# One audio-tower layer on one core: the shared expert fed from stored transposed halves, early output rows, and a new order of the first stage

## What is computed

```
h = gelu(x[:, 1:] @ W1 + x[:, :1] @ W2 + b)               # W = tok_W, 512 x 256
z = layernorm(h);   q, k, v = z Wq^T, z Wk^T, z Wv^T       # 16 heads of 64
h = h + softmax(q k^T / 8) v Wo^T + bo                     # 255 keys
z = layernorm(h);   probs = softmax(z @ router)            # 8 experts, best two, not rescaled
routed = sum over the two of prob_e * (silu(z @ w1[e]) @ w2[e])
shared = sigmoid(z @ gate_w) * ((silu(z @ gate) * (z @ up)) @ down)
out = h + routed + shared                                  # 16 x 255 x 256
```

## Time and profile before

| | |
|---|---|
| three runs | 1058.63, 1057.09, 1057.47 us; median 1057.47 |
| the profiled execution | 1057.78 us, its span 1056.0 us, mean granted PE clock 0.993 |
| busy: PE / PE weight load | 1010.3 us (96%) / 875.0 us (83%) |
| busy: DVE / ACT / POOL | 741.5 (70%) / 660.6 (63%) / 510.8 us (48%) |
| instructions | 23175 |
| moved by DMA | 65.91 MB, 36.09 MB read from HBM and 28.33 MB written |

### The profile page before, as it was taken

How to read it: one execution, slowest core, us unless ns; L and a number is a source line. 1 busy time by engine, 2 the same in 40 slices (tenths; PEclk the granted TensorE clock), 3 DMA queues, 4 the chain that set the end, 5 groups by cost and what they waited for, 6 DMA issues and landing times.

```text
span 1056.0 us, 23175 instructions
## 1 busy us (share of the span) xinstructions
PE 1010.3 (96%) x8042; PEld 875.0 (83%) x8042; DVE 741.5 (70%) x1912; ACT 660.6 (63%) x1939; POOL 510.8 (48%) x557
## 2 busy tenths in 40 slices
PE   6979999999999999999999999999998889999996
PEld 5867888888888888888888888888876779998985
DVE  3757775787688578767857876775783766666677
ACT  4657884787578478757847775784783555554541
POOL 0016543557365455736645573664444486444420
PEclk9999999999999999999999999999999999999998
DMA  8210000001000000100000010000021834444479
GB/s 269 71 46 2 1 2 1 21 1 42 21 1 22 21 21 2 42 21 2 21 22 21 1 42 21 1 22 21 22 70 62 265 89 139 133 142 122 127 225 318
DMA packets 47496, 65.91 MB, mean 62 GB/s; under 512 B 7992, under 2 KB 39480, under 8 KB 47384
## 3 DMA queue, kind: packets, MB, share of 16 engines
q1 hardware_dynamic: 40056, 44.50, 13.5%
q0 software_dynamic: 7056, 19.93, 5.6%
q10 hardware_dynamic: 272, 0.00, 0.0%
HBM read 36.09 MB, written 28.33 MB: 61 GB/s over the span
## 4 chain that ended last, share of the span: by engine, by line
PE 73%; DVE 9%; DMA 4%; ACT 4%; issue 2%; SPq 2%; POOL 0%; DVEq 0%; ACTq 0%; POOLq 0%
PE proj_ps L70 12%; PE proj_ps L72 12%; PE proj_ps L71 12%; PE pT_ps L731 10%; PE proj_ps L744 10%; PE s_ps L713 8%; DMA back<-expert_out_rows 2%; ACT prob L1041 2%; DMA xg<-expert_in_rows 2%; PE s_ps L70 2%; PE s_ps L72 2%; PE s_ps L71 2%; PE s_ps L963 1%; PE pT_ps L984 1%; DVE z L1389 1%
## 5 line engine op out<-in xcount | busy, mean ns | idle before, releaser
L1041 ACT ACTIVATE prob<-s_ps,nmax 128x255 f32<-128x255 f32 x512 | 237.8, 479 | 140.5 <-DVE nmax L1263 139.5
L1720 POOL TENSOR_SCALAR prob<-prob,rinv 128x255 f32<-128x255 f32 x128 | 138.4, 1081 | 258.5 <-DVE rinv L1281 258.0
L1263 DVE TENSOR_REDUCE nmax<-s_ps 128x2 f32<-128x510 f32 x256 | 159.2, 679 | 23.2 <-PE s_ps L713 22.7
L731 PEld LDWEIGHTS pT_ps<-ident,prob 128*128 128x128 f32 x1024 | 114.6, 140 | 37.3 <-issue 29.1
L731 PE MATMUL pT_ps<-ident,prob 128*128 128x128 f32 x1024 | 136.9, 276 | 3.6 <-ACT probT L1067 3.3
L744 PE MATMUL proj_ps<-probT,v 128*64 128x256 f32 x1024 | 125.1, 386 | 2.1 <-DVE probT L1288 2.1
L1722 POOL TENSOR_SCALAR prob<-prob,rinv 128x255 f32<-128x255 f32 x128 | 119.2, 931 | 0.0
L1270 DVE TENSOR_TENSOR qk_space<-proj_ps,qk_space 128x512 fp32r<-128x512 f32 x128 | 87.6, 685 | 38.2 <-ACT qk_space L1053 37.8
L1048 ACT ACTIVATE prob<-prob,rinv 128x255 f32<-128x255 f32 x128 | 67.3, 526 | 66.7 <-DVE rinv L1281 66.5
L713 PE MATMUL s_ps<-qk_space 64*128 64x256 f32 x1536 | 108.3, 287 | 0.4 <-DVE qk_space L1270 0.3
L1041 ACT ACTIVATION_READ_ACCUMULATOR prob<-s_ps,nmax 128x1 f32 x512 | 108.5, 212 | 0.0
(11 more groups left out here) (261 smaller groups left out, 2697.5 us busy)
## 6 DMA issues: line engine op xcount, KB each, us to landing
xg<-expert_in_rows SPq DMA_DIRECT2D x71, 130.0 KB
back<-expert_out_rows SPq DMA_DIRECT2D x6, 1024.0 KB, 21.6
xin<-in_x_dram SPq DMA_DIRECT2D x8, 512.0 KB, 4.6
z_rows<-z SPq DMA_DIRECT2D x8, 512.0 KB, 3.2
z<-z_rows SPq DMA_DIRECT2D x8, 512.0 KB, 4.4
expert_in_rows<-bo_row SPq DMA_DIRECT2D x16, 128.0 KB
raw_up<-in_L_ffn_w_dram SPq DMA_DIRECT2D x8, 256.0 KB, 5.4
raw_down<-in_L_ffn_w_dram SPq DMA_DIRECT2D x8, 256.0 KB, 6.1
```

The source lines that it names most:

```text
L731: m = pe.transpose(pT_ps[h][:, o:o + P], prob[u_par(u)][:, h, qt, kt * P:(kt + 1) * P], ident[:])
L1041: m = act.activation(prob[u_par(u)][:, h, qt, 1:N], s_ps[b][h][:, qt * N + 1:(qt + 1) * N], ACT.Exp, bias=nmax[b][:, n:n + 1], accum_out=r ...
L1263: dve.tensor_reduce(nmax[b][:, 2 * h:2 * h + 2], s_ps[b][h][:].rearrange("p (q k) -> p q k", q=2)[:, :, 1:N], AX_X, ALU.max, negate=True). ...
L1720: pool.tensor_scalar(prob[k][:, 0, 1, 1:N], prob[k][:, 0, 1, 1:N], rinv[k][:, 1:2], None, ALU.mult).then_inc(s_nA1, 1)
```

## The change

1. **Rows.** `x` is read, and `out` written, with tokens 2p and 2p+1 of a sequence on partition p, where they were p and p+128. `store_group` has two transfers of 2 KB per partition and sequence pair and one tiny one (the odd row of partition 0), instead of three of 1 KB rows.
2. **First stage.** SP loads `x(0)` first, then `ro`, then the token weights in two halves of 256 KB, and puts `x(2)`, `x(3)`, `x(4)` behind wq, wk, wv. PE transposes x(0) before `ro`, and the bias matmuls stand behind the 12 matmuls of group 0. DVE takes `tokw_lo` and x(0)'s low halves first.
3. **Passage.** `transpose_z`, `zT_hi` and `zT_lo` of group 0 go to the end of the token stage, behind the last weight banks and ahead of the last rows.
4. **Stored halves.** SP stores `z2T_hi` and `z2T_lo` (256 KB each) instead of `z2`; ACT's `z2_hi` waits for the store of the group before, and DVE's normalisation of `z2` waits for POOL's scatters itself, so `s_z2_free` goes. `load_z3(g)` loads the two halves straight into one of four pairs of buffers, and `transpose_z3`, `z3_hi` and `z3_lo` go everywhere. `load_z3(4)` to `(7)` stand behind `load_x(12)` to `(15)` in SP's queue; they stood before `fill_up`, behind it, behind the 71 loads, and between two `load_back`.
5. **Early output rows.** In the last group the first half of the output projection is done in parts: head pairs 0 to 4 between the probability transposes of round 6, pair 5 and pair 6 around the last transposes of round 7, pair 7 after one `hidden_part`. `split_shared_lo` on DVE moves ahead of the last `probT_b`.

```diff
-    x_rows = x.rearrange("b (h p) d -> p (b h) d", p=P)
+    x_rows = x.rearrange("b (p h) d -> p b (h d)", p=P)
-        z_dram = nc.dram_tensor("z_rows", (GROUPS, P, GT, D), F32).ap()
+        z_dram = nc.dram_tensor("z_columns", (GROUPS, 2, P, DC, GR), F32).ap()
...
+            load_x(0)
             sp.dma_start(ro[:], x[:, 0, :]).then_inc(s_ro, 16)
-            sp.dma_start(tokw[:], tok_w.rearrange("(c p) e -> p c e", p=P)).then_inc(s_tokw, 16)
-            sp.dma_start(xin[0][:], x_rows[:, 0:GT, :]).then_inc(x_in[0], 16)
-            sp.dma_start(xin[1][:], x_rows[:, GT:2 * GT, :]).then_inc(x_in[1], 16)
+            for n in range(2):
+                sp.dma_start(tokw[:, n * DC:(n + 1) * DC, :],
+                             tok_w[n * D:(n + 1) * D, :].rearrange("(c p) e -> p c e", p=P)).then_inc(s_tokw[n], 16)
+            load_x(1)
             for i, w in enumerate((wq, wk, wv)):
                 sp.dma_start(raw[i][:], w.rearrange("(r p) d -> p r d", p=P)).then_inc(s_raw[i], 16)
+                load_x(2 + i)
...
             for g in range(GROUPS):
                 group(g, g == GROUPS - 1)
                 weights(g)
+                if g == GROUPS - 1:
+                    transpose_z()
                 rows(g)
...
+            def store_z2T(r):
+                sp.wait_ge(s_zl2, DC * r + DC)
+                sp.dma_start(z_dram[r, 0], f32(z2T_hi[:])).then_inc(s_zst, 16)
+                sp.dma_start(z_dram[r, 1], f32(z2T_lo[:])).then_inc(s_zst, 16)
...
             def load_z3(g):
-                if g == 0:
+                if g == 2:
                     sp.wait_ge(s_zt, DC * GROUPS)
-                elif g >= 2:
-                    sp.wait_ge(s_zt3, DC * (g - 1))
-                sp.dma_start(z3[g % 2][:], z_dram[g]).then_inc(s_z3_in[g % 2], 16)
+                    sp.wait_ge(s_o, ROUNDS * GROUPS - 1)
+                elif g == 6:
+                    sp.wait_ge(s_scat, 16 * GT * TOP * GROUPS)
+                elif g == 7:
+                    sp.wait_ge(s_zst, 32 * GROUPS)
+                    sp.wait_ge(s_gu, 2 * FC * 4)
+                elif g >= 3:
+                    sp.wait_ge(s_gu, 2 * FC * (g - 2))
+                for part in range(2):
+                    sp.dma_start(f32(z3T[Z3_AT[g]][part][:]), z_dram[g, part]).then_inc(s_z3_in[Z3_AT[g]], 16)
...
             for n in range(RUN):
                 load_x(n)
+                if 2 * BUFS <= n < 2 * BUFS + GROUPS - 4:
+                    load_z3(n - 2 * BUFS + 4)
...
                     transpose_p(g, 2 * p)
+                    next_qk(g, p, first, last)
+                    if last and p == ROUNDS - 2:
+                        pe.wait_ge(s_ve, ROUNDS * GROUPS)
+                        output_part(g, range(0, 5))
+                    elif end:
+                        output_part(g, range(5, 6))
+                    transpose_p(g, 2 * p + 1)
                     if end:
-                        transpose_z3(0)
-                    next_qk(g, p, first, last)
-                    transpose_p(g, 2 * p + 1)
+                        output_part(g, range(6, 7))
...
                     hidden_part(0, 0, 0)
+                    output_part(g, range(7, 8))
+                    output_tile(2, True)
+                    output_tile(3, True).then_inc(s_wo, 1)
                     hidden_part(0, 1, 0)
-                    output_rows(g, 0, True)
-                    output_rows(g, 1, True)
...
             def z2_hi(r, c):
+                if c == 0 and r:
+                    act.wait_ge(s_zst, 32 * r)
...
             def normalise_rows(r):
-                dve.wait_ge(s_z2_free, r + 1)
+                if r:
+                    dve.wait_ge(s_scat, 16 * GT * TOP * r)
```

More of the change, by code:

```diff
@@ L537, in main_phase, with out_ps @@
         FREE_W = 2
+        def out_ps(j, last):
+            return proj_ps[j if last else 1 - j]
         def rows_T_ps(c, last):
@@ L1144, in hidden_split_hi @@
                 act.wait_ge(s_prod, FC * g + c + 1)
-                if g >= 2:
+                if g == 1 and c == 0:
+                    act.wait_ge(s_zst, 32 * GROUPS)
+                elif g >= 2:
                     act.wait_ge(s_rows, 2 * (g - 1))
@@ L1510, in group @@
                             row_slots(r)
+                    if last and p == ROUNDS - 1:
+                        split_shared_lo()
                     if p == ROUNDS - 1 and g + 2 < GROUPS:
@@ L1518, in group @@
                         qk_lo(to, 2 * pair + 1)
-                    if last and p == ROUNDS - 1:
-                        z3_lo(0)
                     probT_b(g, 2 * p + 1)
```

228 lines of the change are left out of this document (97 added, 131 removed).

## The result

| | before | after |
|---|---|---|
| five runs, median (lowest to highest) | 1057.47 us (1054.96 to 1059.23) | 1048.92 us (1047.30 to 1050.61) |
| the profiled execution, its span | 1057.78, 1056.0 us | 1047.30, 1045.6 us |

The ratio of the times is 0.9925, with a 95% interval of 0.9907 to 0.9942: faster by 8 us (7.9 by the ratio, 8.5 by the medians). Forecast were 1044.0 us and a range up to 1048.7. The direction was right, the gain was 8.5 us instead of 13.5, and the median lies 0.2 us outside the range.

A forecast was written before the change was run, and what follows sets the result against it. PE was taken as the bound, carrying 73% of the chain's span. The terms sum to -13.45 us from the profiled 1057.78, giving 1044.3, and 0.3 less against the median: 1044.0 us, range 1040.3 to 1048.7.

The forecast's parts named there:

- First stage, -1.2: First 20 us: x(0) loaded first lets GELU's second pair end at 17.05 instead of 18.26; ends -0.55 and -1.9.
- Passage, -1.95 and -1.2: Token stage to attention, near 62 us: first projection 1.95 us earlier, and 1.2 us more because PE's clock holds.
- a chance of 0.22 that it falls: Rival at the passage: PE's clock falls anyway and six matmuls stay slow, +1.2, 1045.2 us; chance 0.22.
- Last group to first expert, -8.8: From 785 to 858 us: last addition 6.1 us earlier, DVE's work before `fill` 2.4 shorter, 0.3 from reordering.
- early rows pushing the end: Rival in the last group: early output rows delay the last value product by 3.6 us, not 1.0; 1046.6 us, chance 0.13.
- a change that doesn't reach the end: Rival: the 8.8 us before the experts are taken back by other waits, leaving -4.65; 1052.8 us, chance 0.04.
- Expert stage, +2.0: Among the 71 expert tiles: four loads, taken as 512 KB each, overfill the queue and cost 2.0 us; ends 0 and 6.0.
- Queue full (0.13): Rival in the expert stage: each load pushes PE by all its data time, 6.0 us in all; 1048.0 us, chance 0.13.
- The slower case (0.03): Rival in the expert stage: each load holds PE for its whole landing, 16.4 us instead of 2.0; 1058.4 us, chance 0.03.
- Tail, -2.3 with the scatter in it: Last 45 us: last scatter earlier by 0.6, loads of expert rows done 1.5 sooner, stores 0.2 shorter.
- the steady attention costs nothing: Attention from about 90 to 785 us: left alone, its eight stores taken to carry the same bytes, cost nothing.

The follow-up runs named there:

- e4: The kernel before with only the change's first three parts (rows, first stage, passage): 1052.09 us.
- e9: The change, but only the high halves of groups 4 to 7 loaded, 512 KB per load: 1044.26 us.
- e14: The change with seven tile buffers instead of six, the four loads still behind tiles 12 to 15: 1042.49 us.
- e13: The kernel before with seven tile buffers and nothing else: 1051.25 us.
- e3: The change without the loads of halves 4 to 7, those groups computed from older halves in the buffers: 1041.08 us.
- e2: The change with the four loads of halves spread behind tiles 12, 24, 36 and 48: 1052.66 us.
- e7: The change with the four loads at about tiles 12, 24, 36 and 48, issued on ACT's own queue: 1056.44 us.
- e11: The change with seven tile buffers and the four loads of halves right behind the first seven tile loads: 1038.69 us.

## Why the prediction was right and where it failed

- **First stage, -1.2: right; more in the profiled execution.** The product of group 0 starts at 8.83 (said 8.3). In the profiled execution the bias matmuls ended by 14.2 and GELU at 16.2 instead of 17.05: -2.1, beyond the end of -1.9. The reason is the pace within the product: the matmuls are 0.43 us apart at first and 0.23 from 12 us on, while I had them at the slow pace throughout. I take this for the clock; the profile's granted clock reads 1.00 there at either pace, also where the prediction speaks of a low clock in this stage. In the eight traces without this turn, or with it at the very end, GELU ends at 16.9 to 17.5, around the 17.05. That the sum met it owes something to luck: its better end doesn't follow from its terms (13.5, half of 1.73 and 0.6 are 14.97, not 14.45), and the middle would be 17.3.
- **Passage, -1.95 and -1.2: right, the second not always.** The first projection is 4.1 us earlier with the two first terms together at 3.15 forecast, the excess being the first stage's. The clock held in the profiled execution, and this gave 1.3; in eight of thirteen traces it did not. I had put this as one question with one answer (a chance of 0.22 that it falls); it differs from one execution to the next. e4 measures both places together: -4.8 against the kernel before in the same rounds (1052.1 against 1056.8), forecast -4.35. The Trainium skill ("TensorE: Matmul & The Clock Gate", "Part 4: PE-mode transpose") says that transposes don't count as busy in the same way as matmuls; by that this term would be 0. The eight traces in which the granted clock fell (to 0.50 to 0.54 in 2 us windows) agree, the five in which it stayed at 1.00 don't: the transposes and the idle time ahead are the same in both.
- **Last group to first expert, -8.8: nearly.** The early piece held the transposes as worked out; the last value product came 1.2 us later, said 1.0. The last addition came 5.8 us earlier than the earlier stages alone explain, said 6.1. `fill` came 8.2 earlier, said 8.8. The first scatter came 7.4 earlier: here PE waited for POOL (1.82 us before 841.22), which I had named as next in line but expected to be done 1 us before SP. The rivals on this stage, early rows pushing the end (0.13) and a change that doesn't reach the end (0.04), did not come.
- **Expert stage, +2.0: this is the step that failed.** Taken as "four loads of halves, 512 KB each", the excess over the tile loads' time came to 1.3 us, and the worst end to 6.0. The loads are 1 MB each, and the medians give **+7.8** (in the trace, 6.1 at the place itself). The mis-sized term is the bytes, wrong by two. For the assumed bytes the price of 2.0 was about right: e9 has 2.0 at the place and 3.2 in the medians, within the noise of the two. Had I counted the bytes of both halves, the same sum would have read 3.4 + 12.0 - 8.1 = 7.3, with 12.0 as its worst end: near what was measured. A lead one tile too short isn't the reason: with a seventh buffer the loads cost as much at their place (e14), although the stage around them had lost 6.3 us to that lead already in the kernel before (e13). This one term accounts for the miss: 5.8 us more here, 0.95 less in all the others (e3), 4.9 in all.
- **Queue full (0.13)** had 1048.0 us against 1048.9 measured. That is near by luck: its 6.0 us stood for all the data time of 2 MB, and with 4 MB the same rival would have said 12. Kept at its size, it meets a cost of half the data time. The slower case (0.03), 3.9 us for each load, wasn't reached: 2.0 each.
- **Tail, -2.3 with the scatter in it.** The stretch behind the last scatter is 1.3 us shorter, forecast 1.7. That the steady attention costs nothing held too, with twice the bytes stored: from the first projection to the value row near 705 us it takes 641.0 us where it took 642.3, and the difference is the clock at its start.
- **Spread.** The prediction took the profiled execution as standing 0.3 us beside the median. It does for the kernel before, not for the change (1.6 below), and it is not a size to rely on: the runs lie up to 8.2 us apart in e2 and 8.6 in e7.

## What to carry to other kernels

Before pricing a transfer that is moved, count its bytes from shape and type, on both sides of the diff; a stored pair of split halves is twice the fp32 original, and work taken off the engines (here PE, ACT and DVE) is paid for in the queue. A stream of small loads with a fixed number of buffers can be short of lead although the average DMA share is only 0.42: test one buffer more early, because it was worth 6 us here on either kernel. It doesn't make room for megabytes put into the stream; their place does that. And look for the stretch in which the stream's queue is idle because all its buffers are full: with seven buffers 4 MB went through there for almost nothing (a stage of 129.4 us in e11, 129.0 in e13, which has no such loads), giving 1038.7 us against 1057.5 and 1048.9.

## What was not expected of the hardware

- The same loads issued on ACT's queue instead of SP's cost more, 1056.4 against 1052.7 us, with 11.0 us of waits for tiles instead of 7.6. A queue of its own did not shield the stream.
- Cutting 1 MB into four pieces did not help (1050.5 us; ten waits, 10.1 us in all).
- One buffer more gave 6 us, and none of it at the loads that had seemed to need it (14.07 and 14.37 us over the same four tiles).
- After an idle time of PE of 2.9 us at the same place of the program, the granted clock fell to 0.50 to 0.54 in eight executions and stayed at 1.00 in five. In the five, the matmuls of the first product had turned from 0.43 to 0.23 us apart by 13.1 us; in the eight, later.
